# A relational graph layer with a routed feed-forward block: the node features leave on-chip memory, and their place becomes a deeper ring for gathered rows

## What is computed

```python
h = LN(x)
msg = einsum('ni,rio->rno', h, weight)[edge_type, src]
agg = segment_sum(msg, dst, 6250)
x1 = x + agg * 0.5**0.5 + h_bias + (h @ loop_weight) * 0.5**0.5
z = LN(x1)
w = z @ wr + br
sel = indices of the 3124 largest w          # half of the nodes, less one
y[sel] = (gelu(z[sel] @ w1 + b1) @ w2 + b2) * w[sel]
out = x1 + (z + y)                           # y is 0 for nodes not in sel
```

## Time and profile before

| | us |
|---|---|
| median of 3 runs | 2651.34 |
| lowest, highest | 2637.15, 2664.45 |
| profiled execution, first to last instruction | 2726.1 |
| head, until the first gather | 75.3 |
| rounds, first gather to the last one | 2542.7 |
| tail, after the last gather | 108.1 |

### The profile page before, as it was taken

How to read it: one execution, slowest core, us unless ns; L and a number is a source line. 1 busy time by engine, 2 the same in 40 slices (tenths; PEclk the granted TensorE clock), 3 DMA queues, 4 the chain that set the end, 5 groups by cost and what they waited for, 6 DMA issues and landing times.

```text
span 2726.1 us, 40701 instructions
## 1 busy us (share of the span) xinstructions
PE 1928.1 (71%) x10848; PEld 1705.0 (63%) x10849; DVE 949.5 (35%) x1937; ACT 662.0 (24%) x1005; POOL 1758.0 (64%) x1641
## 2 busy tenths in 40 slices
PE   1478776777777777777677777787867786777671
PEld 0367766666767666666566666666756675666571
DVE  6323333333333433333233332332333333333336
ACT  5022221122222231231222222222222221232130
POOL 2667767776776777666667676666776666666620
PEclk7668888878888888788878887888978788888785
DMA  7423333322333233322223222322332232223212
GB/s 248 132 82 90 87 89 91 88 87 83 87 88 90 85 90 88 89 83 82 83 84 91 85 87 78 88 86 81 90 89 78 83 89 82 84 81 89 83 35 95
DMA packets 105730, 245.07 MB, mean 90 GB/s; under 512 B 28465, under 2 KB 50975, under 8 KB 105715
## 3 DMA queue, kind: packets, MB, share of 16 engines
q0 software_dynamic: 79264, 218.32, 27.7%
q1 hardware_dynamic: 26451, 26.58, 3.1%
HBM read 231.96 MB, written 12.82 MB: 90 GB/s over the span
## 4 chain that ended last, share of the span: by engine, by line
PE 34%; another core or an unknown queue 24%; issue 18%; POOL 9%; DVE 6%; ACT 4%; DVEq 3%; DMA 1%; ACTq 1%; POOLq 0%
PE bank L611 14%; PE bank L631 9%; POOL messages L359 8%; PE bank L659 7%; ACT L498 2%; PE bank L650 1%; DVE sums L931 1%; ACT hidden L498 1%; DVEq L920 1%; PE bank L634 1%; DMA messages<-normed_table,row_slots 1%; DVEq L931 1%; PE bank L642 1%; ACT messages L433 0%
## 5 line engine op out<-in xcount | busy, mean ns | idle before, releaser
L359 POOL DMA_INDIRECT messages<-normed_table,row_slots x1616 | 1743.8, 1079 | 843.1 <-issue 493.1
L611 PE MATMUL bank<-onehot,messages 128*128 128x128 f32 x6464 | 977.4, 305 | 265.4 <-issue 234.3
L611 PEld LDWEIGHTS bank<-onehot,messages 128*128 128x128 f32 x6464 | 900.4, 216 | 330.2 <-issue 321.2
L931 DVE SCALAR_TENSOR_TENSOR sums<-bank,regular,sums 128x256 f32 x808 | 391.1, 484 | 1425.6 <-remote 923.6
L631 PE MATMUL bank<-rel_sb,closed 128*128 128x256 f32 x1568 | 404.7, 410 | 65.0 <-issue 62.8
L631 PEld LDWEIGHTS bank<-rel_sb,closed 128*128 128x128 f32 x1568 | 319.5, 207 | 138.3 <-issue 93.6
L659 PE MATMUL bank<-w_sb,hidden 128*128 128x256 f32 x784 | 262.6, 508 | 173.3 <-ACT hidden L498 158.3
L659 PEld LDWEIGHTS bank<-w_sb,hidden 128*128 128x128 f32 x784 | 201.9, 264 | 228.5 <-issue 187.2
L849 DVE TENSOR_TENSOR onehot<-iota,keys 128x1024 f32<-128x1024 f32 x203 | 249.2, 1227 | 146.7 <-issue 134.2
L650 PE MATMUL bank<-normed_t,w_sb 128*128 128x128 f32 x1568 | 233.6, 314 | 57.3 <-ACT normed_t L491 32.8
L650 PEld LDWEIGHTS bank<-normed_t,w_sb 128*128 128x128 f32 x1568 | 224.9, 230 | 68.7 <-issue 68.1
(11 more groups left out here) (149 smaller groups left out, 546.4 us busy)
## 6 DMA issues: line engine op xcount, KB each, us to landing
messages<-normed_table,row_slots POOLq DMA_INDIRECT x1616
normed_table<-messages SPq DMA_DIRECT2D x7, 896.0 KB, 4.8
normed_x<-normed_table SPq DMA_DIRECT2D x49, 128.0 KB
node_out<-nodes SPq DMA_DIRECT2D x12, 512.0 KB
nodes<-in_x POOLq DMA_DIRECT2D x6, 896.0 KB, 8.9
rel_sb<-in_L_gnn_weight SPq DMA_DIRECT2D x2, 1024.0 KB, 7.1
w_sb<-in_L_ffn_w SPq DMA_DIRECT2D x2, 1024.0 KB
acc<-in_dst SPq DMA_DIRECT2D x1, 768.0 KB
```

The source lines that it names most:

```text
L359: pool.indirect_dma_start(messages[:, u, j * D:(j + 1) * D], None, table, bass.IndirectOffsetOnAxis(ap=row_slots[:, half, u * J + j:u * J ...
L611: last = nc.tensor.matmul(banks[u][:, h * D + k * P:h * D + (k + 1) * P], messages[:, u, j * D + k * P:j * D + (k + 1) * P], onehot[:, u, ...
L931: V.scalar_tensor_tensor(sums[:, :, bass.ds(to[h], W)], banks[u][:, h * D:(h + 1) * D].rearrange("p (n m) -> p n m", m=W), regular[:, 0:1] ...
```

## The change

- `nodes` is gone. The chunks of x are loaded all at once into the memory of `messages` (the last into `closed`), normalised in place and stored from there. x is read again from DRAM one block at a time (`x_block`) when a block follows; x1 + z is written block by block to a buffer in DRAM (`residual`), and read back in 7 pieces in the tail. The output is built in `acc`.
- `messages` has 12 slots (`RING`), three rounds. A group is gathered once PE has summed the group 12 before it.
- The gathers stand one after the other in POOL's list, 1616 of them, without a loop. Their index columns come from `gather_rows` itself: `row_slots`, `refill_rows` and `rows_ready` are gone.
- PE's loop has three rounds per iteration, with one round taken out ahead of it.
- The bias is put into `acc` for all blocks ahead of the rounds by one instruction of ACT, and added from there.
- In the head, DVE, ACT and SP run over the chunks without waiting for a staging buffer, and `index_stage` follows chunk 2's factors.
- The selection's buffers have memory of their own (`routing`); the last stage is written out for 49 blocks.
- `EP` (edges per index column) is 128, as before.

```diff
+    EP = 128
+    GE = J * EP
     SLOTS = 4
+    RD = 3
+    RING = RD * SLOTS
+    ROUNDS = -(-(-(-E // GE)) // SLOTS)
+    PEEL = (ROUNDS - 1) % RD + 1
...
-        nodes = sb("nodes", [P, NB, D])
-        messages = sb("messages", [P, SLOTS, J * D])
+        messages = sb("messages", [P, RING, J * D])
...
+            def next_block(b, rows, of):
+                sp.wait_ge(loop_turned, b)
+                sp.dma_start(normed_x[:, :], table_blocks[b]).then_inc(normed_x_in, 16)
+                sp.wait_ge(agg_taken, b + 1)
+                sp.dma_start(x_block[0:rows, :], of).then_inc(x_block_in, 16)
+            def keep_residual(b):
+                sp.wait_ge(resid_ready, b + 1)
+                sp.dma_start(residual_blocks[b], resid[:, :]).then_inc(resid_stored, 16)
+                sp.wait_ge(resid_stored, 16 * b + 16)
+                sp.sem_inc(resid_free, 1)
+            with sp.Fori(1, NB - 1) as b:
+                next_block(b, P, x_blocks[b])
+                keep_residual(b - 1)
...
+            for u in range(SLOTS):
+                sp.wait_ge(pair_summed[u], ROUNDS)
+            sp.wait_ge(agg_ready, NB + 1)
+            for c in range(NCH):
+                sp.dma_start(chunk_rows[c], residual_chunks[c]).then_inc(resid_in[c], 16)
...
-            def gather_round(i, half):
-                pool.wait_ge(rows_ready, i + 1)
-                for u in range(SLOTS):
-                    if not isinstance(i, int):
-                        pool.wait_ge(pair_summed[u], i)
+            def gather(g):
+                if g >= RING:
+                    pool.wait_ge(pair_summed[g % SLOTS], (g - RING) // SLOTS + 1)
+                for j in range(J):
+                    pool.indirect_dma_start(messages[0:EP, g % RING, j * D:(j + 1) * D], None, table,
+                                            bass.IndirectOffsetOnAxis(ap=gather_rows[0:EP, g, j:j + 1], axis=0),
+                                            bounds_check=last_row).then_inc(gathered[g % RING], 16)
+            pool.wait_ge(stored, 16 * NCH)
+            pool.wait_ge(slab_taken, GT)
+            for g in range(RING):
+                gather(g)
...
+            for g in range(RING, NG):
+                gather(g)
...
+            nc.scalar.activation(acc[:, :, :], bias_b[:, :].unsqueeze(1).broadcast_to([P, NB, D]), ACT.Copy).then_inc(acc_ready, 1)
...
-            with pe.Fori(1, ROUNDS) as i:
-                tensor_round(i, lambda u: sum_pair(i, u))
+            for i in range(1, PEEL):
+                tensor_round(i, lambda u: sum_pair(i, u, i % RD, i // RD))
+            with pe.Fori(0, (ROUNDS - PEEL) // RD) as m:
+                for v in range(RD):
+                    tensor_round(RD * m + PEEL + v, lambda u: sum_pair(RD * m + PEEL + v, u, (PEEL + v) % RD, m + (PEEL + v) // RD))
...
             def ffn_enter(b):
                 dve.wait_ge(agg_ready, b + 2)
+                dve.wait_ge(x_block_in, 16 * b + 16)
...
-                V.tensor_tensor(nodes[:, b, :], x1[:, :], normed[:, :], ALU.add).then_inc(ffn_step, 1)
-                dve.wait_ge(ffn_step, FFN_STEPS * b + 5)
+                dve.wait_ge(resid_free, b + 1)
+                V.tensor_tensor(resid[:, :], x1[:, :], normed[:, :], ALU.add).then_inc(resid_ready, 1)
+                dve.wait_ge(resid_ready, b + 1)
+                dve.sem_inc(ffn_step, 1)
```

More of the change, by code:

```diff
@@ L108, in gnn_ffn_program @@
             for k, n in enumerate((STEPS, STEPS, STEPS, STEPS, STEPS + 3)))
-        stage = messages[:, :, :].rearrange("p s (v d) -> p (s v) d", d=D)
+        ring_rows = messages[:, :, :].rearrange("p s (v d) -> p (s v) d", d=D)
+        closed_rows = closed[:, :, :].rearrange("p k n -> p (k n)").rearrange("p (v d) -> p v d", d=D)
+        chunk_rows = [ring_rows[:, c * CH:(c + 1) * CH, :] for c in range(NCH - 1)] + [closed_rows[:, 0:CH, :]]
         loop_sb = sb("loop_sb", [P, KC, D])
@@ L183, in gnn_ffn_program @@
         edges_in = sem("edges_in")
-        x_in = [sem(f"x_in{i}") for i in range(2)]
+        x_in = [sem(f"x_in{c}") for c in range(NCH - 1)]
         x_last_in = sem("x_last_in")
@@ L272, in _, with store @@
             sp.dma_start(loop_sb[:, :, :], loop_w.rearrange("(k p) o -> p k o", p=P)).then_inc(loop_in, 16)
-            def store(c, u):
+            def store(c):
                 sp.wait_ge(norm_ready, c + 1)
-                sp.dma_start(table_chunks[c], stage[:, u * CH:(u + 1) * CH, :]).then_inc(stored[u], 16)
-            store(0, 0)
-            store(1, 1)
+                sp.dma_start(table_chunks[c], chunk_rows[c]).then_inc(stored, 16)
+            for c in range(NCH - 2):
+                store(c)
             sp.wait_ge(x_last_in, 32)
@@ L285, in _ @@
                              rel_w[:, k * P:(k + 1) * P, :].rearrange("r p o -> p r o")).then_inc(rel_in, 16)
[L286 to L290, removed]
+            for c in range(NCH - 2, NCH):
+                store(c)
             for to, a in ((bias_b, h_bias), (b2_b, b2)):
@@ L597, in _, with sum_pair @@
                 pe.wait_ge(rel_in, 16 * KC)
-                with pe.Fori(0, NG_FULL + 1) as g:
+                with pe.Fori(0, PAIRS_FULL + 1) as g:
                     general_pair(g)
-            def sum_pair(i, u):
+            def sum_pair(i, u, turn, use):
+                slot = turn * SLOTS + u
                 pe.wait_ge(onehot_ready[u // 2], i + 1)
-                pe.wait_ge(gathered[u], 64 * (i + 1))
-                if not isinstance(i, int):
+                pe.wait_ge(gathered[slot], 16 * J * (use + 1))
+                if not isinstance(i, int) or i > 0:
                     pe.wait_ge(sum_taken[u], 2 * i)
@@ L1074, in _ @@
             link(pick_step, V.tensor_tensor(keep[:, :], keep[:, :], above[:, :], ALU.add))
-            def finish(b):
-                at = slice(b, b + 1) if isinstance(b, int) else bass.ds(b, 1)
-                V.scalar_tensor_tensor(nodes[:, b, :], acc[:, b, :], keep[:, at], nodes[:, b, :],
+            for b in range(NB):
+                c, v = b // CH, b % CH
+                if v == 0:
+                    dve.wait_ge(resid_in[c], 16)
+                V.scalar_tensor_tensor(acc[:, b, :], acc[:, b, :], keep[:, b:b + 1], chunk_rows[c][:, v, :],
                                        ALU.mult, ALU.add).then_inc(output_ready, 1)
-            with dve.Fori(0, NB // 4) as q:
-                for v in range(4):
-                    finish(4 * q + v)
-            finish(NB - 1)
 _NAMES = ["x", "src", "dst", "edge_type_8", "L0_gnn_weight", "L0_gnn_h_bias", "L0_gnn_loop_weight",
```

231 lines of the change are left out of this document (106 added, 125 removed).

## The result

In the first comparison the changed kernel took 2785.9 us (median of 4 executions, 2778.7 to 2813.6) and the kernel before 2652.0 us (4 executions, 2637.2 to 2664.5): a ratio of 1.051 [1.045, 1.058], where 2580 us were forecast. Later runs put both kernels beside each other again, and the 5% did not come back.

| comparison | kernel before, us (executions) | changed kernel, us (executions) | ratio |
|---|---|---|---|
| first | 2637 to 2665 (4) | 2779 to 2814 (4) | 1.051 [1.045, 1.058] |
| chip 7 | 2392 to 2406 (13) | 2394 to 2406 (10) | 1.0013 [0.9998, 1.0028] |
| chip 6 | 2392 to 2406 (31) | 2396 to 2407 (10) | 1.0011 [0.9996, 1.0027] |
| chip 6, ten minutes earlier | 2720 to 2749 (3) | not run | |
| chip 13 | 2715.5 (1) | 2686.4 (1) | 0.989, one execution each |

What follows compares the result with a forecast made beforehand. The prediction took PE's own delays to bound the rounds, with POOL mostly waiting for PE. 2726.1 less 61 (gather waits) and 12 (head) gave 2653 us, scaled by 0.9726 to 2580 us; range 2400 to 2665, chance 0.47.

Steps and rivals of the forecast that it cites:

- POOL's floor: Rounds: POOL's own gather work, about 2235 us or 22.1 us per round, the least the rounds could take.
- the 61 us: Rounds: PE's named waits for gathers, 76.1 us less 15 early ones, removed by the deeper ring; bounds 9 and 306.
- the second rival: Rounds: removed gather waits return on the block's chain or as PE delays; only 12 us won, 2640 us scaled; chance 0.20.
- The scaling: Whole kernel: profiled time times 0.9726 (2651.3 timed against 2726.1 profiled) gives the timed runs, 2653 to 2580 us.
- POOL's pace: Rounds: evenly fed, PE keeps its higher clock and rounds fall to POOL's gather time; 2342 to about 2500 us; chance 0.22.
- Head: Before the rounds: looking one chunk ahead brings window stage, last store and first gather sooner; 12 us, bounds 0 and 15.
- Per block: Each of 49 blocks: x load, residual store and extra waits cost 0 to 0.3 us; taken as 0, 15 us kept.
- Tail: After the last gather: reading back 6.4 MB of residual takes 25 us of some 45 available, so it costs 0.
- Bias, unrolled gathers, slab columns: Round 0 hides the 11.5 us bias fill; unrolled gathers gain nothing; slab index columns gain 0, at best a little gelu wait.
- Three-round loop: PE's rounds: a loop of about 1000 instructions instead of about 340 was taken to cost 0.
- The third rival: PE's longer loop is fetched again each iteration, 2 us per exposed piece; two pieces, 132 us, 2709 us scaled; chance 0.11.

## Why the prediction was wrong

**POOL's floor** was right: 22.1 us per round and 2235 us in all were forecast as what POOL could reach, 22.0 and 2223 are what it does free. But the kernel before reaches it already. The factor was the execution: its trace and the runs of the forecast were held up.

**The step that failed** is "if gathers were what it waits for, its waits would name them", and from it the 61 us: that a wait of PE's for rows, once removed, comes off the rounds. It failed twice. Free, PE waits some 450 us for the stream, and the profile names 26 of them as a transfer's; the distance from gather to sum and the run with fewer gathers showed the rest. There the ring is worth 0 because POOL can't go faster. Held up, PE is late for its own reason, as the prediction read it, and its size for the waits was near: 51 us ahead of sums from 150 us on by the distance, where the profile names 8.7. The ring did remove them, but they were replaced, not won: POOL's waiting went from 306 to 446 us where about 240 were forecast, gelu's from 158 to 58, and PE's hold-ups from 375 to 627. In place of 61 us less, the rounds were 34 us longer and the tail 35, between the two profiles. That is the second rival ("PE's delays grow with its density"), but it had a price of 0 for the growth, and its reason is not borne out: at four times the products there were 18 hold-ups. What made them grow stays open. The 252 us of growth can be the difference of two conditions as much as of two kernels; on chip 13 the same program had 426.

**The scaling** of 0.9726 to the timed runs took the profiled execution for a slower one of a single kind. The timed runs were of its kind, 2637 to 2665, and 2398 was outside all that was shown. For the changed kernel timed and profiled execution agree.

**POOL's pace**, the first rival, has the right mechanism for the free executions and the right end: 2408 us unscaled, 2401 measured. But it comes with the condition, to both kernels. Its argument (gaps in the supply make PE late) isn't shown by any run.

**Head**: 12 us forecast, 4.6 measured (first gather at 70.7 against 75.3). The window stage came 10.5 us sooner (53.23 against 63.72), as worked out. What failed is that the last store should follow. With the index stage ahead of four chunks, ACT has nothing from 32.2 to 41.8 us and then is the bound, free execution:

```profile
41.81 0.30 ACT L458 ACTIVATE hidden<-hidden,eps 128x7 f32<-128x7 f32 x1 [9.61 <-DVE hidden L745]
42.19 3.55 ACT L465 ACTIVATE messages<-messages,hidden 128x256 f32<-128x256 f32 x7
...
56.23 3.53 ACT L465 ACTIVATE closed<-closed,hidden 128x256 f32<-128x256 f32 x7
...
62.00:70.00 8.00, 1.75 (x7) 1.22 (x6) 6.78 (x18) 1.62 (x3) 0.00 (x0) 0.50 1.06 308
```

The last store was issued at 59.79, 7.7 us sooner, and the stream's wait for it ended 10.6 us after that where it had been 7.8: the transfers of that stretch run at 308 GB/s. So the order of DVE's work set the one end, and ACT's chunks with the transfers behind them the other.

**Per block** 0 with 15 us kept for the range: 13 us less without it, so the truth lay near the bound. **Tail** 0: right where free, 107.4 us against 107.5 and 107.2 in the kernel before with the slab's columns. Held up it was 143.1 against 107.8 in the first comparison; with a lookahead of four groups it was 112 on chip 13, so most of that seems to be POOL's lead, which ends its last gather earlier beside PE's last sum. **Bias, unrolled gathers, slab columns** 0: right within 0.2% where free (the bias only as part of the whole change). **Three-round loop** 0: right, 10 packets against 6. The third rival's price of 2 to 8 us per iteration was fair, 3.1 where the loop is long enough. The Trainium skill, "Runtime: NRT & Kernel Launch", section "Instruction fetch mechanics", has both numbers weighed in the prediction; its room of 2048 instructions for PE is the one that agrees, with 10 packets at 912 matmuls and loads, 13 at 1296, and 338 at 2064. Its rule that a jump beyond a window of two pages forces a fetch doesn't: the loops of 912 and 1296 are longer than that.

**What stays open.** What holds PE up. It isn't bound to a chip, nor to the changed kernel (before: 405), nor to much work on PE. Whether the 5% of the first comparison has anything to do with the change couldn't be settled: comparisons that would have repeated it landed free, or had one execution of each.

## What to carry to other kernels

A single wait label is no proof of what an engine doesn't wait for: PE's "issue" held some 450 us of waiting for rows, and it took the time from each group's last gather to its sum, and an edit of the supply (three gathers for four), to tell so. Before a wait is taken out, add up the stream that feeds it; if instructions times duration already fill the rounds, as 1616 x 1.375 us do here, a deeper buffer can't help, and where the consumer was late, it only moved the waiting. And run the kernel before beside every experiment: here its time, 2398 or 2720, told which bound was being measured.

## What the runs showed that I had not expected

- The same program on the same chip took 2728 us and ten minutes later 2399. In the slower executions PE starts one matmul per 0.7 us in stretches of some us, its completions reach DVE, ACT and POOL late, and the traces hold some 4.2 to 4.7 semaphore updates per us where the free ones hold 12.8 to 13.5. The Trainium skill, "NOTIFIC — the notification-queue block", section "7.1 Overflow: three behaviours, one of which stalls the engine", says that the recording of events can stall an engine; no run here tests that. The kernel with four times the products, more to record and with as few updates in its trace, had 18 hold-ups.
- A one-row-per-partition gather of 128 x 1 KB costs POOL 1.05 to 1.08 us in the mean and 0.30 us before the next, held up or free, looped or unrolled; it sets 2223 us of 2401.
- PE's instructions are loaded again in each iteration of a loop of 2064 matmuls and loads, for 3.1 us each time, and not in one of 1296.
